# Eleven centering and variance products in two single-rate passes instead of one fp32 pass

## The reference

```python
def _ln_c(v, eps=1e-06):
    m = jnp.mean(v, axis=1, keepdims=True)
    s = jnp.var(v, axis=1, keepdims=True)
    return (v - m) / jnp.sqrt(s + eps)
...
x = x + _L1_conv_ref(_ln_c(x), ...)
t = _to_tokens(x)
t = t + _L1_ffn_ref(_ln_t(t), L1_ffn_Wg, L1_ffn_W1, L1_ffn_W2)   # 8 experts, 512 hidden, silu
x = x + _L2_conv_ref(_ln_c(x), ...)                               # channel gate from pooled means
t = t + _L2_ffn_ref(_ln_t(t), ...)                                # 8 experts, 512 hidden, gelu
x = x + _L3_conv_ref(_ln_c(x), ...)                               # saliency map
t = t + _L3_ffn_ref(_ln_t(t), ...)                                # 8 experts, 256 hidden, relu
```

## Time and profile before

| what | us or share |
|---|---|
| median of the runs (3) | 394.35 |
| the profiled run, its own time | 392.55 |
| its span, first to last instruction | 390.6 |
| TensorE busy (modelled, overlapping) | 375.9 (96%) |
| ScalarE busy | 290.1 (74%) |
| VectorE busy | 259.5 (66%) |
| GpSimd busy | 156.0 (40%) |
| granted TensorE clock, mean | 0.998 of full speed |

### The profile page before, as it was taken

The page is one execution under the profiler, slowest core; times in us unless marked ns, Lnnn a source line. Parts: engine busy times, 40 slices in busy tenths (PEclk is TensorE's granted clock), DMA queues, the critical chain, the costliest instruction groups (busy, mean ns, idle before and its releaser), DMA issues.

```text
span 390.6 us, 5157 instructions
## 1 busy us (share of the span) xinstructions
PE 375.9 (96%) x1666; PEld 274.5 (70%) x1670; DVE 259.5 (66%) x572; ACT 290.1 (74%) x517; POOL 156.0 (40%) x135
## 2 busy tenths in 40 slices
PE   8999999999999999999999999999999999998995
PEld 3688876455567777887777677877777767666783
DVE  0745666945435864785875986758957497677776
ACT  3552456935206778978889889999899998899783
POOL 5413000930298175123575772211233366342244
PEclk9999999999999999999999999999999999999999
DMA  7960000000000145604010030152040112220242
GB/s 246 450 209 1 2 1 2 0 0 2 1 0 0 48 129 216 258 3 134 29 48 5 3 109 27 32 185 80 13 125 29 28 27 77 61 78 3 65 127 82
DMA packets 11020, 28.64 MB, mean 73 GB/s; under 512 B 1247, under 2 KB 2527, under 8 KB 10737
## 3 DMA queue, kind: packets, MB, share of 16 engines
q1 hardware_dynamic: 10992, 28.31, 22.0%
HBM read 27.69 MB, written 0.62 MB: 72 GB/s over the span
## 4 chain that ended last, share of the span: by engine, by line
PE 69%; ACT 17%; DVE 10%; issue 3%; POOLq 0%; POOL 0%; DVEq 0%
PE ps L443 17%; PE ps L444 16%; PE ps L445 16%; ACT hidh L1101 4%; ACT ps L1102 4%; PE ps L450 3%; ACT wb L1068 3%; PE ps L753 2%; PE ps L455 2%; DVE hidl L1476 2%; PE ps L466 1%; ACT rstd L982 1%; ACT rstd L984 1%; PE ps L544 1%; PE ps L647 1%
## 5 line engine op out<-in xcount | busy, mean ns | idle before, releaser
L1476 DVE TENSOR_TENSOR hidl<-ps,hidh 128x512 fp32r<-128x512 f32 x160 | 108.5, 687 | 50.5 <-ACT ps L1102 49.1
L411 POOL TENSOR_TENSOR x<-x,parts 128x512 f32<-128x512 f32 x43 | 56.1, 1304 | 146.8 <-DVE parts L1486 95.7
L443 PE MATMUL ps<-xh,wh_all 128*128 128x512 f32 x160 | 74.2, 464 | 2.2 <-DVE hidl L1476 1.7
L1101 ACT ACTIVATE hidh<-ps,par 128x512 fp32r<-128x512 f32 x96 | 68.1, 710 | 10.4 <-PE ps L445 8.6
L443 PE MATMUL ps<-hidh,wh_all 128*128 128x512 f32 (+1 forms) x162 | 64.2, 396 | 3.0 <-DVE hidl L1476 2.8
L1102 ACT ACTIVATE ps<-ps,par 128x512 f32<-128x512 f32 x96 | 65.3, 680 | 0.0
L444 PE MATMUL ps<-xh,wl_all 128*128 128x512 f32 x160 | 63.4, 396 | 0.0
L444 PE MATMUL ps<-hidh,wl_all 128*128 128x512 f32 (+1 forms) x162 | 63.4, 391 | 0.0
L445 PE MATMUL ps<-hidl,wh_all 128*128 128x512 f32 (+1 forms) x162 | 63.2, 390 | 0.0
L445 PE MATMUL ps<-xl,wh_all 128*128 128x512 f32 x160 | 63.0, 393 | 0.0
L401 POOL TENSOR_TENSOR wl_all<-wa,wh_all 128x512 fp32r<-128x512 f32 x40 | 51.2, 1296 | 3.5
(11 more groups left out here) (261 smaller groups left out, 581.7 us busy)
## 6 DMA issues: line engine op xcount, KB each, us to landing
scores_all<-rows_scratch SPq DMA_DIRECT2D x48, 256.0 KB, 3.4
wa<-in_moe SPq DMA_DIRECT2D x2, 4096.0 KB, 15.4
wa<-in_moe SPq DMA_DIRECT2D x1, 2048.0 KB, 9.1
dft_o<-in_dft_o SPq DMA_DIRECT2D x1, 640.0 KB
w<-in_w_out SPq DMA_DIRECT2D x1, 576.0 KB, 7.4
cst<-in_consts SPq DMA_DIRECT2D x1, 512.5 KB, 6.4
x<-in_x SPq DMA_DIRECT2D x2, 256.0 KB, 3.0
we<-in_w_experts SPq DMA_DIRECT2D x1, 512.0 KB, 8.2
```

The costliest lines, as they stand in the source:

```text
L411: pool.tensor_tensor(half(x, h), half(x, h), parts[:, n % 2, :], ALU.add).then_inc(s["state_added"], 1)
L443: pe.matmul(o, wh, xhi, start=start, stop=False)
L1101: act.activation(hidh[:, n % 2, f, :], sums, func, bias=bias).then_inc(s["hidden_hi_act"], 1)
L1476: dve.tensor_tensor(hidl[:, n % 2, f, :], bank(sums_bank(n, f)), f32(hidh[:, n % 2, f, :]), ALU.subtract).then_inc(s["hidden_lo"], 1)
```

## The change

Eleven of the L450 and L455 products, all in blocks 0 to 3, no longer read fp32 operands. VectorE first writes a rounded pair of the operand into `xh`, `xl` of the same half (a copy and a subtraction, the second one waiting for the first), and TensorE runs two fp32r passes over that pair with a rounded copy of the constant matrices, `norm_w`. The four centers are (3,1), (5,0), (5,1), (7,0); the seven variances (3,1), (4,0), (5,0), (4,1), (5,1), (6,0), (7,0). The pairs of the squares come after `low` of a given chunk, and VectorE waits there for the square; the pairs of the state come after `low(3, 1)` in block 0, behind `gate_half` in blocks 1 and 2, behind `saliency_half` in block 3. TensorE's order of products is unchanged. The `norm_w` copy (128 x 256) stands on VectorE ahead of `mix_half(1)`, in the first layer.

```diff
+        norm_w = sb("norm_w", [C, 2 * C], F32R)
...
+        state_splits = [(3, 1), (5, 0), (5, 1), (7, 0)]
+        square_splits = [(3, 1), (4, 0), (5, 0), (4, 1), (5, 1), (6, 0), (7, 0)]
...
             def center(n, h):
 
+                if (n, h) in state_splits:
+                    pe.wait_ge(s["state_split"], state_splits.index((n, h)) + 1)
+                    pe.matmul(bank(center_bank(n, h)), norm_w[:, 0:C], half(xh, h), start=True, stop=False)
+                    pe.matmul(bank(center_bank(n, h)), norm_w[:, 0:C], half(xl, h), start=False, stop=True).then_inc(s["centered"], 1)
+                    return
                 x_ready(pe, n, h)
...
             def variance(n, h):
 
+                if (n, h) in square_splits:
+                    pe.wait_ge(s["square_split"], square_splits.index((n, h)) + 1)
+                    pe.matmul(bank(variance_bank(n, h)), norm_w[:, C:2 * C], half(xh, h), start=True, stop=False)
+                    pe.matmul(bank(variance_bank(n, h)), norm_w[:, C:2 * C], half(xl, h), start=False, stop=True).then_inc(s["variance"], 1)
+                    return
                 pe.wait_ge(s["squared"], seq(n, h))
...
+            step(dve.tensor_copy(norm_w[:], cst[:, 0:2 * C]))
             mix_half(1)
...
+            def split_state(n, h):
+                if (n, h) in state_splits:
+                    x_ready(dve, n, h)
+                    step(dve.tensor_copy(half(xh, h), half(x, h)))
+                    dve.tensor_tensor(half(xl, h), half(x, h), f32(half(xh, h)), ALU.subtract).then_inc(s["state_split"], 1)
+
+            def split_square(n, h):
+                if (n, h) in square_splits:
+                    dve.wait_ge(s["squared"], seq(n, h))
+                    step(dve.tensor_copy(half(xh, h), work(sq, n, h)))
+                    dve.tensor_tensor(half(xl, h), work(sq, n, h), f32(half(xh, h)), ALU.subtract).then_inc(s["square_split"], 1)
...
+                    elif (n, f) == (3, 1):
+                        split_state(3, 1)
+                    elif (n, f) == (4, 3):
+                        split_square(3, 1)
...
-                        if (j, f) == (1, 3):
+                        if (j, f) == (1, 1):
+                            split_square(4, hh)
+                        elif (j, f) == (4, 3):
+                            split_square(5, hh)
+                        elif (j, f) == (1, 3):
...
                         elif (j, f) == (3, 1):
                             gate_half(hh)
+                            split_state(5, hh)
...
-                    if (j, f) == (1, 3):
+                    if (j, f) == (1, 1):
+                        split_square(6, 0)
+                    elif (j, f) == (3, 3):
+                        split_square(7, 0)
+                    elif (j, f) == (1, 3):
...
                     elif (j, f) == (2, 2):
                         saliency_half(0)
+                        split_state(7, 0)
```

More of the change, by code:

```diff
@@ L90 @@
     "early_x1", "early_centered", "early_squared", "early_variance", "early_log", "early_rstd", "early_normed", "early_hi", "early_lo",
-    "centered", "squared", "variance", "log_var", "rstd", "normed", "norm_hi", "norm_lo",
+    "state_split", "square_split", "centered", "squared", "variance", "log_var", "rstd", "normed", "norm_hi", "norm_lo",
     "dve_step",
```

## The result

The changed kernel took 395.58 us (median of 22 runs, 393.87 to 397.85), the kernel before 394.15 us in the same comparison (22 runs, 391.64 to 396.90): a ratio of 1.0046, 95% interval 1.0025 to 1.0068. By the ratio it is slower by about 1.8 us, half a per cent; the two medians lie 1.4 us apart. The profiled execution took 394.40 us, span 392.5, against 392.55 and 390.6 before.

A forecast was written before the change was run, and what follows sets the result against it. TensorE, 69% of the chain of waits, was taken to set the end. Its 4.4 us saving, less late pairs, GpSimd waits and savings waited away, came to -0.25; against the 394.35 median that gave 394.6 us, range 391.0 to 397.2.

The forecast's parts named there:

- savings and delays within 2 us of each other: Whole kernel: the main forecast, TensorE savings and VectorE delays nearly cancel, 0.25 us slower; chance 0.65.
- The saving of 0.40 per product: TensorE, eleven products: fp32 takes 0.86 us, two fp32r passes 0.46, saving 0.40 each, 4.4 us together.
- The pair of 1.20 us: VectorE: copy 0.48, wait 0.03 and subtraction 0.69 make each pair ready 1.20 us after it starts.
- The three uncovered pairs of the state: Behind the gate in blocks 1 and 2 and in block 3: next low part 0.9, 0.74 and 1.2 us late.
- The `norm_w` copy at nothing: VectorE ahead of L1308: about 0.3 us within 0.70 idle, costing nothing if it gets its turn before GpSimd's L359.
- Rival B: GpSimd takes the turn between copy and subtraction and ahead of the `norm_w` copy: 4.0 us more, 398.6; chance 0.12.
- The squares' pairs in idle time of VectorE: Seven variances: the pairs come where VectorE sits idle; without GpSimd they would cost nothing anywhere.
- GpSimd beside the squares' pairs: Port waits up to 1.3 us; charged 0.25 in block 0, 0.5 and 0.15 at block 2's variances 4 and 5.
- Blocks: Net per block, savings positive: block 0 +0.55, block 1 -0.15, block 2 -0.6, block 3 -0.05.
- Delays as a plain sum: Blocks 0 to 3: savings and late pairs added place by place, giving -0.25 us in all.
- Rival A: TensorE keeps nearly everything, late low parts being absorbed: up to 4.4 us saved, 390.0; chance 0.22.
- C: Rival: the passes are not single rate, each as dear as the fp32 product, adding 9.5 us, 403.8; chance 0.01.

The follow-up runs named there:

- e12: Changed kernel, three state pairs moved to GpSimd, GpSimd held at five squares' pairs and before its `img_f` sum: 0.9977 of the kernel before, full clock 390.9 us.
- e1: Changed kernel with only the seven variance products in two passes, all centers fp32 again: 0.9999 of the kernel before, full clock 393.6 us.
- e3: Changed kernel with the three uncovered state pairs issued one or two chunks later on VectorE: 1.0067 of the kernel before, full clock 395.4 us.
- e4: Changed kernel with the three uncovered state pairs computed on GpSimd: 1.0039 of the kernel before, full clock 394.3 us.
- e8: e1 with GpSimd held at five places until the pair of squares is done: 1.0024 of the kernel before, full clock 393.1 us.
- e11: Changed kernel cut to four centers, four variances; three state pairs on GpSimd, GpSimd held at two squares' pairs and its `img_f` sum: 0.9942 of the kernel before.

## Why the prediction was right, and which of its terms were not

The forecast, savings and delays within 2 us of each other, came true; its size did not: 0.25 us slower predicted, 1.8 to 1.9 measured. 1.07 lies ahead of the mixtures, where nothing was predicted, and 1.13 against 0.25 in them; the closing stretch gives 0.36 back. The stated range, 391.0 to 397.2 us, would have held an unchanged kernel as well, so what the forecast is worth shows in its terms.

- **The saving of 0.40 per product: right.** The ledger drops by 0.39 to 0.41 at each.
- **The pair of 1.20 us: right, slightly high.** The copy is 0.43 (taken 0.48), the subtraction 0.69, as the subtraction of the earlier trace rows.
- **The three uncovered pairs of the state: right.** Predicted 0.9, 0.74, 1.2; measured 1.14, 0.65, 1.18. In the first one, L1624 (0.66 us, until 197.63) waited for GpSimd's L405 (until 197.61), as L1597 had with 0.52 before. So VectorE reached the place 0.79 us later than before and TensorE 0.66 later, which leaves 0.21 us in hand instead of the 0.34 of the earlier trace rows. The pair pushes L1503 back by 1.19, it takes 0.06 from the end of L1503 to the product, and the first product after the idle time takes 0.10 longer: 1.19 - 0.21 + 0.06 + 0.10 = 1.14.
- **The `norm_w` copy at nothing: the step that failed.** At its own place it cost nothing, as predicted: 0.46 us at 31.31 (0.3 taken), ended 0.15 behind GpSimd's L361 (until 31.62) and ahead of its L363, and L1322 (before: L1308) starts at 31.98, no later than the 32.1 named. But I looked for its cost there alone. It came at `filt_two`, 1.07 us, where 0.09 us decided the turn. Rival B had the mechanism, GpSimd taking the port in between, and the wrong place; its sign, waits of over 0.5 us for most of the squares' pairs, came at two of seven.
- **The squares' pairs in idle time of VectorE: right for three of seven.** The other four copies (152.03, 204.69, 260.05, 305.99) start with no idle time ahead of them, and two of these pairs do not fit even without GpSimd, as e12 shows.
- **GpSimd beside the squares' pairs: right in kind, too small.** Block 0's variance 3 lost 0.48 where 0.25 was charged. In block 2, variance 4 got the worse of the two cases that I had averaged: 0.9 against 0.5. VectorE and GpSimd there:
```profile
234.82 0.94 DVE L1497 CAST xh<-sq 128x512 fp32r<-128x512 f32 x1
235.79 1.67 DVE L1498 TENSOR_TENSOR xl<-sq,xh 128x512 fp32r<-128x512 f32 x1
...
234.18 2.73 POOL L405 TENSOR_TENSOR wl_all<-wa,wh_all 128x512 fp32r<-128x512 f32 x2
```
The first L405 ends, the copy gets the port, and before the subtraction is issued the second L405 has it (until 236.91). I called this possible and gave it half; four of the seven pairs of squares have a stretched subtraction (three of 1.67, one of 0.98), and so has the pair of the state in block 0.
- **Blocks.** Savings positive: block 0 +0.30 (predicted +0.55), block 1 -0.90 (-0.15), block 2 -0.72 (-0.6), block 3 and the tail +0.19 (-0.05). Block 1 is the miss. Four terms add to it: the state pair 0.24 more than charged, 0.45 at variance 5 that I let the stretch behind it swallow, 0.27 at the gate's inputs (0.05 charged), and 0.23 at the end of the block: 1.14, less the 0.40 of variance 5, which I had written off. Blocks 2 and 3 have stretches with ScalarE nearly full that take such losses back. The changed kernel's windows (answers to the earlier trace rows; length, then busy PE, PEld, DVE, ACT, POOL):
```profile
250.00:277.00 27.00, 26.18 (x123) 21.04 (x122) 20.74 (x50) 25.39 (x44) 5.17 (x4) 1.00 0.28 99
252.50:279.50 27.00, 26.18 (x116) 20.62 (x115) 22.28 (x57) 26.78 (x45) 5.17 (x4) 1.00 0.28 98
```
At the same times ScalarE is busy 25.39 us instead of 26.83, but these are no longer the same instructions: the window begins ahead of a wait of 1.45 us at the gate. Moved by about the lag, it shows 26.78, as full as before.
- **Delays as a plain sum: right here by luck.** I added the late pairs as if each stood alone. e1, e3 and e4 show that they cover each other: with the pairs of the state gone or moved, the variance pairs behind them cost 1.0 to 2.3 each instead of 0.45 to 0.9.

Rival A is excluded by the three waits, C by the 0.47 us for two passes.

The Trainium skill (SBUF — State Buffer, section Who interferes with whom) describes VectorE and GpSimd sharing SBUF ports under a lock held for a whole instruction. e8 agrees, with 5.8 us of stretched instructions gone once GpSimd is held.

## What to carry to other kernels

Before moving work from a full engine to one with idle time, list who shares a port with the new instructions at each place, count how much is in hand there, and take the worse order where another engine's next instruction is queued: a pair of dependent instructions gives it two openings. Read the cover at each place, not at one for all. Keep only the places with cover and no neighbour; here 6 and 8 products of 11 gain 0.4 and 0.6% at full clock, and all 11, as first placed, lose 0.5%. Look also at every later place where two engines race for a turn by less than 0.1 us, since a single early instruction can flip it.

## What was not expected of the hardware

- One VectorE copy of 128x256 at 31 us made four 128x49 operations at 103 us take 0.91 instead of 0.81 us; a tile of the same size without the copy did not. No run here explains it.
- A small operation waits for GpSimd as a large one does: `filt_two`, 128x196 from SBUF to SBUF, went from 0.43 to 1.50 us for two.
- The runs of the same kernel differ by up to 5 us, and their times go with their mean granted clock. In the profiled runs of eight of the fourteen kernels a spell of half the clock begins at 96 to 98 us, in the third mixer, and lasts 6.8 or 10.2 us; in the others it is missing. The same stretch in e11, with such a spell (granted clock 0.57 over the window), and in the kernel before, without:
```profile
96.00:108.00 12.00, 12.00 (x35) 7.45 (x34) 4.02 (x13) 1.67 (x4) 0.08 (x1) 0.57 0.01 2
```
```profile
96.00:108.00 12.00, 11.55 (x56) 6.64 (x57) 4.72 (x15) 2.27 (x5) 3.43 (x3) 1.00 0.01 2
```
In the same 12 us, 35 matmul records instead of 56. Low mean clocks came in the unchanged kernel and in the variants alike, so I take them for no part of the change's effect; but they cost more than that effect, and the ratios' intervals are wide with them.
